# Silu stage of a fused attention and FFN kernel: the first group's z made within the last attention batches, the second's turned into another PSUM bank ahead of the first products

## The chip, the cores and the metric

The kernel runs on one core of one Trainium2 chip. The metric is the device time of one launch in microseconds (us), the median of several runs; lower is better. The profiled execution is one more run of the same program.

## The reference, cut to what matters

The activations x are 64 tiles of 128 tokens by 128 features. Eight layers follow each other, each of the form x = x + layer(layernorm(x)): a cross attention, a feed-forward network (FFN) with Silu, a cross attention, a quantised FFN, a cross attention, a gated FFN, a wide attention and a routed FFN. The change touches the first attention's last tile group and the first FFN:

```
residual = x                       # x here is already layernorm(x), the outer one
h = layernorm(x) * ln_gamma + ln_beta
w1, w2 = dequant(fc1_q, fc1_scales), dequant(fc2_q, fc2_scales)
y = silu(h @ w1 + fc1_bias)        # 128 -> 512 features
return residual + 0.5 * (y @ w2 + fc2_bias)
```

Because the layer is called on an already normalised x and adds that normalised input back, the kernel adds std2 * z to x as well as the FFN's output.

## The kernel before, in words

x stays in the on-chip memory for the whole kernel. Every layer is a "phase", written as one program for each engine. Phases are strung by one counter: VectorE (DVE) raises `phase_done` at the end of a phase, and the other engines wait for it before they begin the next. Inside a phase, each engine's order is written out by hand and semaphores join them. The tokens are worked in 16 groups of GT = 4 tiles.

**The first attention** works tile by tile (t = 0 to 63). DVE's share of tile t is, in this order (`CrossAttention.vector`, loop `body`): `normalise(t+1)` (row sums L1007, reciprocal L1009, scaling L1012, probabilities L1015), `shift(t+2)` (maxima L996, differences L999), `residual(t)` (L1021, which waits for TensorE's weighted sum of tile t, L780), then the statistics of tile t-1 for the next layer (`next_stats.tile`, L283 and L285). In the last group (t = 60 to 63, k = 0 to 3) it also calls `SiluFfn.prepare(k)`, which dequantises the FFN's weights: k = 0 scales fc1 (L1409), k = 1 fc2 and the bias (L1412 to L1416), k = 2 splits w1 into a high and a low part (L1418, L1420), k = 3 makes the bias rows (L1423 to L1431). After the loop come the statistics of tile 63, then `phase_done`. In this last group ScalarE (ACT) has one exponential for each tile (L924) and copies the turned probabilities (L916). TensorE (PE) turns the probabilities (L753) and sums them (L780).

**The Silu FFN** (`SiluFfn`, a `Hidden`) works group by group. For group g:

- DVE makes z = (x - mean) * rstd, four instructions at L346 (`vector_z`), into the one buffer `core.z`.
- PE turns z, four transposes at L1188 (`turn_z`), into PSUM bank 5.
- ACT copies it out with gamma and beta (L1256, `copy_zt`) into the one buffer `zt`; it waits until the group before has been split.
- DVE splits it in two (L1291, L1293, `split_zt`) and adds std2 * z to x, four instructions at L356 (`vector_once`, called by `keep_once`).
- PE multiplies with w1, three passes for each of four chunks: 12 matmuls at L87, L88, L89 (`hidden`), into banks 0 to 3.
- ACT applies Silu, four times L1267 (`activate`). The first of them brings a load of the function table.
- PE adds the bias by one matmul (L1441) and multiplies with w2 by 32 matmuls at L1216 (`output`), into bank 6 or 7 (`obank`).
- DVE adds the result to x (L1306, `add_output`).

TensorE's order in the steady state is: `hidden(g+1)`, `turn_z(g+2)`, `output(g)`. Ahead of it stand, in `tensor_walk`, `turn_z(0)`, `hidden(0)`, `turn_z(1)`. ACT's prologue is `copy_zt(0)`, `activate(0)`, `copy_zt(1)`. DVE's is `vector_z(0)`, `split_zt(0)`, `keep_once(0)`, `vector_z(1)`, `split_zt(1)`, `keep_once(1)`. In this layer `turn_gates`, `apply_gates` and `vector_stats` do nothing; the gated FFN, the only other `Hidden`, has its own order and its own `turn_z` and `copy_zt`.

The next attention's weights are asked for by SyncE (SP, L660) as soon as the first attention is done, so the first of these four requests also marks the moment of `phase_done`.

Of the kernel before, what the change touches and what calls it, by code (L numbers as in the profile page):

```python
# [34 lines left out]
P = 128  # L35
# [38 lines left out]
def for_groups(eng, body, peel=1):  # L74


    with eng.Fori(0, GROUPS // 2 - peel) as i:
        body(2 * i, 0, 2 * peel)
        body(2 * i + 1, 1, 2 * peel)
    for left in range(2 * peel - 1, -1, -1):  # L80
        body(GROUPS - 1 - left, 1 - left % 2, left)
# [389 lines left out]
class CrossAttention(Phase):  # L471
# [267 lines left out]
    def turn_z(self, eng, g, u, slot):  # L739
        c = self.core  # L740
        eng.wait_ge(self.ln.z_ready.sem, self.ln.z_ready.at(GT * g + GT))
        eng.wait_ge(self.t_copied.sem, self.t_copied.free(u))
        for k in range(GT):
            mm = eng.transpose(c.ps_t[:, slot, k * P:(k + 1) * P], c.z[:, k, :], c.ident[:, :])
        mm.then_inc(self.t_done.sem, 1)
# [153 lines left out]
    def copy_zt(self, eng, par, u, slot):  # L899
        c = self.core  # L900
        eng.wait_ge(self.t_done.sem, self.t_done.at(u + 1))
        if self.affine:
            eng.activation(self.zt[:, par, :], c.ps_t[:, slot, :], ACT.Identity,
                           scale=self.gb[:, 0:1], bias=self.gb[:, 1:2]).then_inc(self.t_copied.sem, 1)
        else:
            eng.activation(self.zt[:, par, :], c.ps_t[:, slot, :], ACT.Copy)\
               .then_inc(self.t_copied.sem, 1)
# [234 lines left out]
class Hidden(Phase):  # L1142
# [38 lines left out]
        return self.core.bank(6 + par)  # L1181


    def turn_z(self, eng, g, par):
        c = self.core
        eng.wait_ge(self.ln.z_ready.sem, self.ln.z_ready.at(GT * g + GT))
        for k in range(GT):
            mm = eng.transpose(c.bank(5)[:, k * P:(k + 1) * P], c.z[:, k, :], c.ident[:, :])  # L1188
        mm.then_inc(self.zt_turned.sem, 1)

    def hidden(self, eng, g, par, first=False):
# [35 lines left out]

    def tensor_walk(self, eng):
        self.turn_z(eng, 0, 0)
        self.hidden(eng, 0, 0, True)  # L1230
        self.turn_gates(eng, 0, 0, range(5))
        self.turn_z(eng, 1, 1)

        def step(g, par, left):
            if left > 0:
                self.hidden(eng, g + 1, 1 - par)
                self.turn_gates(eng, g + 1, 1 - par, (0, 1))
            if left > 1:
                self.turn_z(eng, g + 2, par)
            self.output(eng, g, par, (0, 1))  # L1240
            if left > 0:
                self.turn_gates(eng, g + 1, 1 - par, (2, 3))
            self.output(eng, g, par, (2, 3))
            if left > 0:
                self.turn_gates(eng, g + 1, 1 - par, (4,))

        for_groups(eng, step)


    def copy_zt(self, eng, g, par, first=False):  # L1250
        if not first:
            eng.wait_ge(self.zt_split.sem, self.zt_split.at(g))
        eng.wait_ge(self.zt_turned.sem, self.zt_turned.at(g + 1))
        src = self.core.bank(5)
        if self.affine is not None:
            ins = eng.activation(self.zt[:, :], src, ACT.Identity, scale=self.affine[:, 0:1],  # L1256
                                 bias=self.affine[:, 1:2])
        else:
            ins = eng.activation(self.zt[:, :], src, ACT.Copy)
        ins.then_inc(self.zt_copied.sem, 1)  # L1260
# [8 lines left out]

    def scalar_walk(self, eng):  # L1270
        self.copy_zt(eng, 0, 0, True)
        self.activate(eng, 0, 0, True)
        self.copy_zt(eng, 1, 1)

        def step(g, par, left):
            if left > 0:
                self.activate(eng, g + 1, 1 - par)
            if left > 1:
                self.copy_zt(eng, g + 2, par)
                self.stage_gates(eng, g + 2, par)  # L1280

        for_groups(eng, step)
# [28 lines left out]
            self.ln.vector_once(eng, g, par)  # L1311

    def vector_walk(self, eng):
        self.ln.vector_z(eng, 0)
        self.split_zt(eng, 0, 0)
        self.ln.vector_stats(eng, 1)
        self.keep_once(eng, 0, 0)
        self.ln.vector_z(eng, 1)
        self.apply_gates(eng, 0, 0)
        self.split_zt(eng, 1, 1)  # L1320
        self.ln.vector_stats(eng, 2)
        self.keep_once(eng, 1, 1)

        def step(g, par, left):
            if left > 1:
                self.ln.vector_z(eng, g + 2)
            if left > 2:
                self.ln.vector_stats(eng, g + 3)
            if left > 0:
                self.apply_gates(eng, g + 1, 1 - par, (0, 1))  # L1330
            if left > 1:
                self.split_zt(eng, g + 2, par)
            if left > 0:
                self.apply_gates(eng, g + 1, 1 - par, (2, 3, 4))
            if left > 1:
                self.keep_once(eng, g + 2, par)
            self.add_output(eng, g, par)

        for_groups(eng, step, 2)
        eng.wait_ge(self.added.sem, self.added.at(GROUPS))  # L1340
        eng.sem_inc(self.done.sem, 1)
# [11 lines left out]
class SiluFfn(Hidden):  # L1353
# [50 lines left out]
    def prepare(self, eng, k):  # L1404

        p, c = self.prep, self.core
        if k == 0:
            eng.wait_ge(self.loaded.sem, self.loaded.at(16 * 8))
            eng.scalar_tensor_tensor(out=self.s1[:], in0=self.q1[:], scalar=-128.0, in1=self.s1[:], op0=ALU.add,  # L1409
                                     op1=ALU.mult).then_inc(p.sem, 1)  # L1410
        elif k == 1:
            eng.scalar_tensor_tensor(out=self.s2[:], in0=self.q2[:], scalar=-128.0, in1=self.s2[:], op0=ALU.add,  # L1412
                                     op1=ALU.mult).then_inc(p.sem, 1)
            eng.tensor_scalar(self.bias[:, :], self.bias[:, :], 0.5, None, ALU.mult).then_inc(p.sem, 1)
            eng.wait_ge(p.sem, p.at(3))
            eng.tensor_scalar(self.s2[:], self.s2[:], 0.5, None, ALU.mult).then_inc(p.sem, 1)  # L1416
        elif k == 2:
            eng.tensor_copy(self.w1[0][:], self.s1[:]).then_inc(p.sem, 1)  # L1418
            eng.wait_ge(p.sem, p.at(5))
            eng.tensor_tensor(self.w1[1][:], self.s1[:], self.w1[0][:].bitcast(F32), ALU.subtract)\  # L1420
               .then_inc(p.sem, 1)
        else:
            eng.tensor_copy(self.bias_high[:, :], self.bias[:, :]).then_inc(p.sem, 1)  # L1423
            eng.tensor_scalar(self.ones[:, :], c.ident[:, :], 0.0, 1.0, ALU.mult, ALU.add).then_inc(p.sem, 1)
            eng.wait_ge(p.sem, p.at(8))
            high = self.bias_high[:, :].bitcast(F32)
            eng.tensor_tensor(self.bias_low[:, :], self.bias[:, :], high, ALU.subtract).then_inc(p.sem, 1)
            eng.tensor_scalar(self.bias_row[:, :], high, c.ident[:, 0:1], None, ALU.mult).then_inc(p.sem, 1)
            eng.wait_ge(p.sem, p.at(10))
            spread = lambda a: a[:, :].unsqueeze(1).broadcast_to([P, GT, P])  # L1430
            eng.scalar_tensor_tensor(out=self.bias_rows[:, :, :], in0=spread(self.bias_low),  # L1431
                                     scalar=c.ident[:, self.LOW:self.LOW + 1], in1=spread(self.bias_row),
                                     op0=ALU.mult, op1=ALU.add).then_inc(p.sem, 1)
# [25 lines left out]
class QuantFfn(Phase):  # L1459
# [278 lines left out]
    def tensor(self, eng):  # L1738
# [19 lines left out]
        def hidden(g, par, first=False):  # L1758
            eng.wait_ge(self.zqt_ready.sem, self.zqt_ready.at(g + 1))
            for k in range(C):  # L1760
                if not first:
                    eng.wait_ge(self.act_done.sem, self.act_done.at(C * (g - 1) + k + 1))
                eng.matmul(c.bank(k), self.wt[:, 0, k, :], self.zqt(par),
                           start=True, stop=True).then_inc(self.hid_done.sem, 1)

        turn_z(0, 0)
        turn_z(1, 1)
        hidden(0, 0, True)
        turn_z(2, 0)

        def step(g, par, left):
# [528 lines left out]
class WideAttention(Phase):  # L2300
# [74 lines left out]
    def tensor(self, eng):  # L2375
# [35 lines left out]
        def means(g):  # L2411

            self.tail.wait(eng, g)
            for k in range(GT):
                b = GT * g + k
                eng.matmul(c.bank(self.MEANS_BANK)[:, BANK - BATCH + b:BANK - BATCH + b + 1],
                           c.x[:, b, :], self.tail.rstd[:, b:b + 1], start=True, stop=True)

        prepare(0, 0, True)
        scores(0, 0, True)  # L2420

# [118 lines left out]
class RoutedFfn(Phase):  # L2540
# [254 lines left out]
    def scalar(self, eng):  # L2795
        c, U, A = self.core, self.U, self.AHEAD
        eng.wait_ge(self.before.sem, self.before.at(1))
        def copy_zt(g, par, first=False):
# [3 lines left out]
            eng.activation(self.zt[:, par, :], c.bank(6 + par), ACT.Copy).then_inc(self.zt_copied.sem, 1)  # L2802

        copy_zt(0, 0, True)
        sc = self.score[:, 0, :]
        eng.wait_ge(self.exp_go.sem, self.exp_go.at(1))
# [23 lines left out]
        def step(g, par, left):  # L2830
            for j in range(U):
                u = U * g + j
                if j < U - A or left > 0:
                    gelu(u + A, j + A)
                if j < U - A + 1 or left > 0:
                    scaled(u + A - 1, j + A - 1)
                if j == 2 and left > 0:
                    copy_zt(g + 1, 1 - par)
# [249 lines left out]
```

## Time and profile before

| | |
|---|---|
| median of 3 runs | 2571.04 us (2566.32 to 2573.92) |
| the profiled execution, whole | 2571.09 us |
| its span | 2569.3 us |
| mean granted TensorE clock | 0.939 of full speed |
| PE busy | 2287.2 us, 89% |
| DVE busy | 1869.3 us, 73% |
| ACT busy | 1459.9 us, 57% |

The span runs from the profile's first to its last instruction; some 1.8 us of the execution lie outside it. A share of busy time is a mean over all stages. The first attention ends and the Silu FFN begins near 683 us.

### The profile page before, as it was taken

Reading aid. Unit: us, or ns where it says so; the run is one execution under the profiler, and the core shown is the slowest. Engines: PE = TensorE matmul, PEld = TensorE weight load, DVE = VectorE, ACT = ScalarE, POOL = GpSimd, SP = SyncE. Lnnn points to the kernel's source line nnn. Section 1 sums busy time; section 2 is a strip of 40 time slices with the busy share of each in tenths; the row PEclk is TensorE's granted clock in tenths of the full one; section 3 lists DMA queues with packets and bytes.
Section 4 is the critical chain, followed back from the end, with each engine's and each line's share of the span. In section 5 each row is a group of like instructions: output and inputs, shape, how many; then the busy total and the mean of one; then the engine's idle time right before and its main releaser. Section 6 shows DMA issues by size and latency. Waiting matters only on the chain.

```text
span 2569.3 us, 49258 instructions
## 1 busy us (share of the span) xinstructions
PE 2287.2 (89%) x14961; PEld 1969.9 (77%) x14962; DVE 1869.3 (73%) x4436; ACT 1459.9 (57%) x2849; POOL 513.8 (20%) x700
## 2 busy tenths in 40 slices
PE   7899999999798999952458999999996998979997
PEld 6788888888597888841146888888885787879997
DVE  3778878778754888877873778888886665756665
ACT  5455565555344566624776666666663563646665
POOL 2022222222101121101001111111112341412333
PEclk9999999999899999985658999999998999989999
DMA  8444454444101444420013554545541000024444
GB/s 207 114 132 123 121 147 125 131 139 125 54 0 51 123 131 136 138 61 1 0 34 101 148 146 137 147 139 139 139 125 45 1 1 14 27 61 132 131 131 136
DMA packets 460456, 256.53 MB, mean 100 GB/s; under 512 B 25440, under 2 KB 441468, under 8 KB 460348
## 3 DMA queue, kind: packets, MB, share of 16 engines
q1 hardware_dynamic: 460348, 255.27, 35.9%
q8 instruction: 46, 0.75, 0.1%
q14 instruction: 62, 0.51, 0.1%
HBM read 150.10 MB, written 105.12 MB: 99 GB/s over the span
## 4 chain that ended last, share of the span: by engine, by line
PE 71%; DVE 13%; ACT 6%; issue 6%; POOL 1%; DVEq 1%; DMA 1%; ACTq 0%; SPq 0%; POOLq 0%
PE ps_o L780 11%; PE ps_s L764 11%; PE ps_p L87 6%; PE ps_p L88 6%; PE ps_p L89 6%; PE ps_t L753 6%; PE ps_o L1216 3%; PE ps_t L1216 2%; DVE a_sm L1007 2%; DVE a_e L1015 2%; DVE a_mx L996 2%; PE ps_s L87 2%; PE ps_t L2767 2%; PE ps_o L2767 1%; PE ps_s L89 1%
## 5 line engine op out<-in xcount | busy, mean ns | idle before, releaser
L780 PEld LDWEIGHTS ps_o<-a_val,a_pt 128*128 128x128 f32 (+2 forms) x3200 | 414.7, 193 | 35.0 <-issue 9.2
L764 PE MATMUL ps_s<-a_keys,a_zt 128*128 128x308 f32 (+1 forms) x1024 | 419.3, 494 | 14.5 <-ACT a_keys L879 6.8
L780 PE MATMUL ps_o<-a_val,a_pt 128*128 128x128 f32 (+2 forms) x3200 | 425.5, 276 | 6.7 <-ACT a_pt L916 3.9
L1007 DVE TENSOR_REDUCE a_sm<-a_e 128x16 f32<-128x1232 f32 (+1 forms) x192 | 234.3, 1220 | 226.7 <-ACT a_e L924 224.8
L888 ACT ACTIVATE a_stage<-ps_p 128x512 f32<-128x512 f32 (+1 forms) x370 | 221.1, 598 | 290.9 <-PE ps_p L89 289.8
L916 ACT ACTIVATE a_pt<-ps_t 128x512 f32<-128x512 f32 (+1 forms) x448 | 225.4, 505 | 161.7 <-PE ps_t L753 161.3
L879 ACT ACTIVATE a_keys<-ps_p 128x308 f32<-128x308 f32 x603 | 257.4, 427 | 102.5 <-PE ps_p L89 102.3
L996 DVE TENSOR_REDUCE a_mx<-ps_s 128x6 f32<-128x462 f32 (+1 forms) x512 | 255.5, 548 | 62.1 <-PE ps_s L764 41.1
L753 PE MATMUL ps_t<-ident,a_e 128*128 128x128 f32 (+1 forms) x1600 | 262.2, 276 | 31.6 <-DVE a_e L1015 29.2
L87 PE MATMUL ps_p<-ct_hi,a_mt_hi 96*128 (+1 forms) x603 | 258.9, 429 | 0.0
L1015 DVE TENSOR_TENSOR a_e<-a_e,a_rs 128x1232 f32<-128x1232 f32 (+1 forms) x192 | 251.7, 1311 | 6.6
L999 DVE TENSOR_TENSOR a_e<-ps_s,a_mx 128x462 f32<-128x462 f32 (+1 forms) x512 | 253.7, 545 | 0.0
L924 ACT ACTIVATE a_e<-a_e 128x1232 f32<-128x1232 f32 (+1 forms) x192 | 204.2, 1064 | 74.5 <-DVE a_e L999 72.4
L753 PEld LDWEIGHTS ps_t<-ident,a_e 128*128 128x128 f32 (+1 forms) x1600 | 194.8, 140 | 41.4 <-DVE a_e L1015 20.5
L764 PEld LDWEIGHTS ps_s<-a_keys,a_zt 128*128 128x128 f32 x1024 | 168.8, 190 | 42.3 <-issue 16.8
L87 PE MATMUL ps_p<-a_vo_hi,a_windowhi 96*128 96x512 f32 (+1 forms) x370 | 191.0, 516 | 0.0
L89 PE MATMUL ps_p<-ct_hi,a_mt_lo 96*128 (+1 forms) x603 | 184.2, 305 | 0.0
L88 PE MATMUL ps_p<-ct_lo,a_mt_hi 96*128 (+1 forms) x603 | 183.8, 305 | 0.0
L208 POOL TENSOR_TENSOR ln_var<-ln_mean_var,eps 128x4 f32<-128x4 f32 x48 | 9.6, 201 | 719.2 <-DVE ln_mean_var L195 710.2
L88 PE MATMUL ps_p<-a_vo_lo,a_windowhi 96*128 96x512 f32 (+1 forms) x370 | 146.9, 397 | 0.0
L89 PE MATMUL ps_p<-a_vo_hi,a_windowlo 96*128 96x512 f32 (+1 forms) x370 | 146.4, 396 | 0.0
L87 PEld LDWEIGHTS ps_p<-ct_hi,a_mt_hi 96*128 96x128 f32 x603 | 115.1, 191 | 39.3 <-issue 30.5
(392 smaller groups left out, 4675.3 us busy)
## 6 DMA issues: line engine op xcount, KB each, us to landing
a_vals<-a_stage SPq DMA_DIRECT2D x160, 512.0 KB, 3.5
a_val<-a_vals SPq DMA_DIRECT2D x128, 576.0 KB
f_w<-in_L_ffn_W_dram SPq DMA_DIRECT2D x129, 256.0 KB, 2.6
a_vals<-a_stage SPq DMA_DIRECT2D x40, 416.0 KB
a_val<-a_vals SPq DMA_DIRECT2D x64, 256.0 KB
a_val<-a_vals SPq DMA_DIRECT2D x128, 40.0 KB
x<-in_x_dram SPq DMA_DIRECT2D x8, 512.0 KB, 7.6
out_dram<-x SPq DMA_DIRECT2D x8, 512.0 KB, 5.4
```

What stands on the lines that cost most here:

```text
L87: eng.matmul(out, lhs[0], rhs[0], start=start, stop=False)
L88: eng.matmul(out, lhs[0], rhs[1], start=False, stop=False)
L89: return eng.matmul(out, lhs[1], rhs[0], start=False, stop=stop)
L753: mm = eng.transpose(c.ps_t[0:w, slot, (i % GT) * P:(i % GT + 1) * P], src[:, P * i:P * i + w], c.ident[:, :])
L764: mm = eng.matmul(o, zt, keys[:, h0:h0 + nh, :], start=True, stop=not self.masked)
L780: mm = eng.matmul(c.ps_o[:, (i % 2) * P:(i % 2 + 1) * P], self.pt[0:r, n, :], self.val[0:r, i % 2, n, :], start=(n == 0), stop=(n == self. ...
L879: eng.activation(self.keys[:, par, :, h, :], bank[:, 0:GCOLS].rearrange("p (b k) -> p b k", b=GT), ACT.Copy)\
L916: mm = eng.activation(dst[:, i0:full, :], src[:, 0:full - i0, :], ACT.Copy)
L996: eng.tensor_reduce(self.mx[:, h0:h0 + nh], bank, AX.X, ALU.max).then_inc(self.max_ready.sem, 1)
L999: eng.tensor_tensor(dest, src, bc(self.mx[:, h0:h0 + nh], KEYS), ALU.subtract)\
L1007: eng.tensor_reduce(self.sm[:, :], e, AX.X, ALU.add).then_inc(st.sem, 1)
L1015: eng.tensor_tensor(e, e, bc(self.rs[:, :], KEYS), ALU.mult).then_inc(self.probs_ready.sem, 1)
```

## The change

`prepare(1)` also makes z of group 0; `prepare(2)` also adds std2 * z to group 0's x and takes over all that `prepare(3)` did; `prepare(3)` is empty. In the Silu FFN, group 1's z is turned into bank 7 (`obank(1)`) instead of bank 5, and its place on all three engines moves ahead of the first products: TensorE turns group 1 before `hidden(0)`, ACT copies it before `activate(0)`, and DVE makes z of group 1 as soon as group 0 is turned, before it splits group 0.

```diff
+    def tbank(self, g):
+
+        return self.obank(1) if isinstance(g, int) and g == 1 else self.core.bank(5)
+
     def turn_z(self, eng, g, par):
...
-            mm = eng.transpose(c.bank(5)[:, k * P:(k + 1) * P], c.z[:, k, :], c.ident[:, :])
+            mm = eng.transpose(self.tbank(g)[:, k * P:(k + 1) * P], c.z[:, k, :], c.ident[:, :])
...
     def tensor_walk(self, eng):
         self.turn_z(eng, 0, 0)
+        self.turn_z(eng, 1, 1)
         self.hidden(eng, 0, 0, True)
-        self.turn_gates(eng, 0, 0, range(5))
-        self.turn_z(eng, 1, 1)
...
     def copy_zt(...)
-        src = self.core.bank(5)
+        src = self.tbank(g)
...
     def scalar_walk(self, eng):
         self.copy_zt(eng, 0, 0, True)
+        self.copy_zt(eng, 1, 1)
         self.activate(eng, 0, 0, True)
-        self.copy_zt(eng, 1, 1)
...
     def vector_walk(self, eng):
-        self.ln.vector_z(eng, 0)
+        eng.wait_ge(self.zt_turned.sem, self.zt_turned.at(1))
+        self.ln.vector_z(eng, 1)
         self.split_zt(eng, 0, 0)
-        self.ln.vector_stats(eng, 1)
-        self.keep_once(eng, 0, 0)
-        self.ln.vector_z(eng, 1)
-        self.apply_gates(eng, 0, 0)
         self.split_zt(eng, 1, 1)
-        self.ln.vector_stats(eng, 2)
         self.keep_once(eng, 1, 1)
...
     def prepare(self, eng, k):       # k == 1, at its end
             eng.tensor_scalar(self.s2[:], self.s2[:], 0.5, None, ALU.mult).then_inc(p.sem, 1)
+
+            self.ln.vector_z(eng, 0)
         elif k == 2:
+            self.keep_once(eng, 0, 0)
             eng.tensor_copy(self.w1[0][:], self.s1[:]).then_inc(p.sem, 1)
...
-        else:
             eng.tensor_copy(self.bias_high[:, :], self.bias[:, :]).then_inc(p.sem, 1)
```

## Rows read from the trace of the kernel before

**Rows 1.** The page's first part: busy time, share, instructions of each engine.
```profile
PE 2287.2 (89%) x14961; PEld 1969.9 (77%) x14962; DVE 1869.3 (73%) x4436; ACT 1459.9 (57%) x2849; POOL 513.8 (20%) x700
```
**Rows 2.** Chain that ended last, 640 to 730 us: start, us, what.
```profile
671.25 0.43 DVE f_w L1416
671.67 1.36 DVE a_sm L1007
...
695.85 0.50 PE ps_s L87
```
**Rows 3.** Timeline of DVE, 668 to 706: start, us, instruction, idle before it.
```profile
676.02 0.69 DVE L1420 TENSOR_TENSOR f_w1lo<-f_s,f_w1hi 128x512 fp32r<-128x512 f32 x1
680.51 0.29 DVE L1021 TENSOR_TENSOR x<-ps_o,x 128x128 f32<-128x128 f32 x1 [3.79 <-PE ps_o L780]
...
681.13 0.19 DVE L1423 CAST f_b_high<-f_b 128x128 fp32r<-128x128 f32 x1
...
682.69 0.28 DVE L283 BATCH_NORM_STATS2 tail_stats<-x 128x6 f32<-128x128 f32 x1
...
683.21 1.11 DVE L346 TENSOR_SCALAR z<-x,tail_mean_var,tail_rstd 128x128 f32<-128x128 f32 x4
686.48 0.43 DVE L1291 CAST f_zthi<-f_zt 128x512 fp32r<-128x512 f32 x1 [2.16 <-ACT f_zt L1256]
...
687.55 1.13 DVE L356 SCALAR_TENSOR_TENSOR x<-z,a_std,x 128x128 f32<-128x128 f32 x4
688.79 1.11 DVE L346 TENSOR_SCALAR z<-x,tail_mean_var,tail_rstd 128x128 f32<-128x128 f32 x4
```
**Rows 4.** Timeline of PE, 675 to 706.
```profile
676.93 3.54 PE L780 MATMUL ps_o<-a_val,a_pt 128*128 128x128 f32 x20
684.46 1.09 PE L1188 MATMUL ps_t<-ident,z 128*128 128x128 f32 x4 [3.99 <-DVE z L346]
687.69 0.79 PE L87 MATMUL ps_s<-f_zthi,f_w1hi 128*128 128x512 f32 x1 [2.14 <-DVE f_ztlo L1293]
...
692.98 0.61 PE L1188 MATMUL ps_t<-ident,z 128*128 128x128 f32 x4
695.85 0.50 PE L87 MATMUL ps_s<-f_zthi,f_w1hi 128*128 128x512 f32 x1 [2.27 <-DVE f_ztlo L1293]
...
700.30 0.60 PE L1188 MATMUL ps_t<-ident,z 128*128 128x128 f32 x4
```
**Rows 5.** Timeline of all engines, 655 to 716.
```profile
664.03 2.39 PE L780 MATMUL ps_o<-a_val,a_pt 128*128 128x128 f32 x20
...
683.07 0.35 SPq L660 DMA_DIRECT2D a_wq<-in_L_xattn_Wq_dram  x1
...
704.47 0.48 PE L87 MATMUL ps_s<-f_zthi,f_w1hi 128*128 128x512 f32 x1
...
707.35 0.60 PE L1188 MATMUL ps_t<-ident,z 128*128 128x128 f32 x4
```
**Rows 6.** Timeline of ACT, 668 to 706.
```profile
669.92 1.23 ACT L924 ACTIVATE a_e<-a_e 128x1232 f32<-128x1232 f32 x1 [0.68 <-DVE a_e L999]
...
685.67 0.78 ACT L1256 ACTIVATE f_zt<-ps_t,f_gb 128x512 f32<-128x512 f32 x1 [8.06 <-PE ps_t L1188]
689.42 1.28 ACT L1267 ACT_TABLE_LOAD   x1 [2.97 <-PE ps_s L89]
...
693.18 0.69 ACT L1267 ACTIVATE f_hid<-ps_p,f_b 128x512 f32<-128x512 f32 x1 [0.55 <-PE ps_p L89]
```
**Rows 7.** Windows: stretch, length, busy of each engine, granted clock, DMA share, GB/s.
```profile
689.50:693.00 3.50, 3.50 (x10) 2.56 (x9) 0.41 (x2) 3.11 (x4) 0.00 (x0) 0.50 0.00 0
693.00:696.40 3.40, 1.13 (x7) 0.83 (x6) 1.80 (x5) 1.36 (x2) 0.00 (x0) 1.00 0.00 0
696.40:699.80 3.40, 3.40 (x9) 2.64 (x8) 1.53 (x6) 1.52 (x3) 0.00 (x0) 0.50 0.03 7
...
701.00:800.00 99.00, 99.00 (x691) 90.16 (x690) 53.98 (x150) 44.42 (x71) 0.00 (x0) 1.00 0.00 0
```

## The prediction, made before the changed kernel ran

> **What bounds the kernel now.** The page's busy shares come first: TensorE is busy 89% of the span and DVE 73% [rows 1]. That is a mean over eight stages, and the change touches one seam, so the stage's own rows decide. I read the chain that ended last around 683 us, then the timelines of DVE, PE and ACT one by one, then the granted clock by windows.
>
> Three regimes meet at the seam. In the attention's last tiles the chain runs through DVE: the fc2 scaling of `prepare(1)` ends, and the row sums of tile 63 start at once behind it [rows 2]. Tile 63's exponential had ended at 669.92 + 1.23 = 671.15 [rows 6], so those row sums wait for DVE's queue and not for ACT. Then comes a prologue in which one engine at a time works. From 701 us on PE is busy in all of the 99.00 us looked at, at full clock [rows 7]: there nothing but PE's own work sets the pace: 99.00 us for 691 matmuls at 49 a group (12, 4, 1 and 32) is 7.0 us a group. So microseconds won before 701 reach the stage's end whole; the steady state has no slack on PE to swallow them. The next stage begins when this one ends, and its weights are asked for at the seam, over 100 us ahead of their use, so it moves with it.
>
> **The change, part by part.** I keep the times of the profiled execution and say what each edit adds to or takes from the path.
>
> *1. z of group 0 in `prepare(1)`.* Four instructions at L346 take 1.11 us [rows 3]. They go in between the end of L1416 and the row sums of tile 63, on the path, where nothing covers them: the exponential is only some 0.4 us ahead of its use. Cost +1.1. The inputs (x and the statistics of group 0) have been ready for long, so it waits for nothing. Behind it in DVE's queue stand tile 63's row sums and probabilities, and PE waits for these: its turned probabilities and the last weighted sum move by 1.1 too. Bounds: +0.7, if the 0.4 hid a part, which the chain speaks against, and +1.2.
>
> *2. `keep_once(0)` and the bias rows in `prepare(2)`.* DVE ends L1420 at 676.71 and then stands idle 3.79 us until PE's last weighted sum lets the residual go at 680.51 [rows 3]. Into that gap go four L356 (1.13 us) and the old `prepare(3)`, which lasts from 681.13 to 682.69, 1.56 us [rows 3]: 2.7 us of work. The weighted sum moves by the same 1.1 as the start of the gap, so the gap keeps its 3.8 us and 1.1 us are left over. Cost nothing. Without that cover, whatever runs over 3.8 us would delay the residual one for one; if the sum ended 1.05 us sooner (20 matmuls in 2.39 us as at 664 instead of 3.54 [rows 4, 5]), it would just fit.
>
> *3. `prepare(3)` empty.* It stands between the statistics of tile 62 and those of tile 63, all on the path. Gain 1.56, from 681.13 to 682.69 [rows 3].
>
> *4. `vector_z(0)` off the seam.* Before, the stage was declared done by 683.07, when SP issues its first request [rows 5], and the first transpose came at 684.46 [rows 4], behind z. Now z is there already, and PE begins about as soon as SP did, give or take a tenth: 683.2 to 683.3. Gain 1.2 (1.1 to 1.4).
>
> *5. `vector_z(1)` ahead of `split_zt(0)`.* The transposes of group 0 end at 685.55; ACT's copy runs 685.67 to 686.45 and the split follows at 686.48 [rows 3, 6]. DVE now waits for the end of the transposes too and spends 1.11 us on z of group 1, so the split begins about 1.25 behind the transposes' end instead of 0.93. Cost +0.3, between nothing and 0.5. The new wait for `zt_turned` holds only work that depends on it anyhow. The second transposes, 1.09 us at half clock, end within a tenth of the split's own end, so `hidden(0)` behind them on PE hardly waits.
>
> *6. The stall between `hidden(0)` and `hidden(1)`.* Call the start of `hidden(0)` X; before it is 687.69. `hidden(0)` runs to X + 5.3 = 692.98; then come four transposes, an idle 2.27 us, and `hidden(1)` at 695.85 [rows 4]. The idle time is one engine after another: transposes, copy at 693.8 once the four Silu are done, split. Now ACT copies group 1 at X (it waits for the first split), to X + 0.8; DVE splits to X + 2.0. That is 3.3 us before PE needs it. ACT's Silu of group 0 are not later, since the table load waits for the first chunk at X + 1.73 [rows 6] and the copy is over by X + 0.8. So `hidden(1)` follows `hidden(0)` directly. Gain 695.85 - 692.98 = 2.87. It also needs Silu (0, c) for chunk c: 1.28 of table load and four of 0.69 (pitch 0.64) from X + 1.73 put the last at X + 5.7 to 6.2, chunk by chunk ahead of PE. `output(0)`, `turn_z(2)` and `split_zt(2)` keep their old distance behind `hidden(1)`, and z of group 2 is ready by X + 4.4.
>
> *7. The clock.* `hidden(0)` still had 0.50 in the row up to 693.0; from there it was 1.00, when PE had been busy without a gap for 5 us, and 0.50 again from 696.4, after the idle gap before `hidden(1)`; from 699.8 it stays 1.00 [rows 7]. These are the levels 1.2 and 2.4 GHz. `hidden(1)` took 700.30 - 695.85 = 4.45 us [rows 4]; the same twelve matmuls at full clock take 707.35 - 704.47 = 2.88 [rows 5]. With no gap before it the clock should not fall again. Gain 1.57. `hidden(0)` itself took 5.29 where full clock takes 2.88, so it could gain from 0 to 2.4 if the clock rises sooner; since PE now does the second transposes just ahead of it, some 1.2 us more of gapless work, I take a rise 1.2 us earlier, which is worth 1.2 x (5.29 - 2.88) / 5.29 = 0.5.
>
> The trace thus has the clock fall after a gap and rise after gapless work. The Trainium skill (TensorE: Matmul & The Clock Gate, Part 1) says the same, but adds that the moment is run-variable, so that one kernel shows a different number of slow matmuls from run to run, and warns against fitting a specific count. By the rows the clock gives 2.1 us; by the page that term should be left unsized, and the sum would be 2.1 smaller. One trace cannot show how it varies.
>
> *The last attention tile.* PE's idle time before tile 63 grows from 2.5 to 3.6 us. Its weighted sum already ran mostly at half clock, 3.54 us against 2.39 [rows 4, 5]; all at half clock, by the ratio 5.29 / 2.88 that item 7 gives, it would take 4.39, so it may lose up to 0.85, or gain up to 1.15. The middle is near nought, which I take.
>
> **Sum:** +1.1 - 1.56 - 1.2 + 0.3 - 2.87 - 1.57 - 0.5 = -6.3 us. Against the profiled execution's own 2571.09, which stands at the runs' median of 2571.04, that is **2564.8 us**.
>
> **The rivals.**
>
> *A, the clock gives more.* `hidden(0)` mostly at full clock (another 1.9) or the last weighted sum at full clock (1.1). For it: nothing but 1.2 us of transposes now lies before X and no gap. Against: the same gapless stretch needed 5 us before. Time about 2562.5.
>
> *B, the stall stays.* The second split comes late, because ACT's copy waits for the first split, the turn waits for z, and each sits in a hand-written queue; PE then still idles before `hidden(1)` and the clock falls again. Only items 1 to 5 count: -1.4, so 2569.7. Against it stand 3.3 us of slack.
>
> *C, DVE's new load at the seam costs more.* The four L356 and the bias rows, with their waits, outlast the gap, or the small instructions do not fit in: 1 to 2 us late, so 2566.5. Against it: 1.1 us left over.
>
> *D, slower.* The granted clock stays at half through the whole prologue and two outputs. PE's longer gap before tile 63 leads in, and the full clock that PE had from 693.0 to 696.4 is lost. Price: `hidden(0)` and `hidden(1)` at half are 10.6 us instead of the 7.7 of the sum, 2.9 more. Transposes, bias and the 32 matmuls of an output take 704.47 - 700.30 = 4.17 us at full clock [rows 4, 5], and by the ratio 1.84 another 3.5 at half. It decides for slower only once the half clock lasts to X + 18, the end of the first output: 2.9 + 3.5 just makes up for the 6.3. Through the next group too (2.4 + 3.5) it gives 2577, while nothing in the trace has PE busy that long at half.
>
> **How the numbers follow.** Chances: the forecast (5 to 7.7 us less) 0.48, A 0.27, B 0.11, C 0.10, D 0.04. 0.3% is 7.7 us, about what a measurement of this kernel can tell from no change. The forecast falls 1.4 us short of it; the three runs of before lie 7.6 us apart, so about a quarter of the forecast's share and most of A's come out beyond it: faster 0.36. B, C and the rest of the forecast are within: 0.60. Slower 0.04. The range goes from A with both clock terms, 2561.8, to B, 2569.7, each widened for the spread of a median: 2559 to 2570.5. It leaves out D and the far tails of A.
>
> **What would show it.** Right: no L1423 to L1431 after the last residual, and these with four L356 in DVE's gap before it; the first L1188 within 0.3 us of SP's first request; eight L1188 before the first L87; 24 matmuls L87 to L89 without a gap, the later twelve in about 2.9 us; first L1441 some 8.5 us behind X instead of 13. Wrong: idle time before `hidden(1)`; a granted clock of 0.50 in it; a residual of tile 63 that starts well behind the end of PE's last sum; a second table load; a group period other than 7 us after the prologue.

## The result, and the profile after

The changed kernel takes 2562.67 us (median of 7 runs, 2556.63 to 2565.35), against 2571.49 us for the kernel before (7 runs): 8.8 us less. The ratio is 0.9964, 95% interval 0.9951 to 0.9977, that is 0.23% to 0.49% less time. Forecast were 2564.8 us and 6.3 less; the range held the time. The likeliest single case was "within 0.3%"; the ratio lies just beyond that bound and its interval reaches to both sides of it. The 8.8 us also lie outside the forecast's own band of 5 to 7.7 us less, and the median stands at rival A's 2562.5.

I measure the change by a **seam** that every profile shows: from the start of tile 61's residual (the third last L1021) to the first addition of an FFN output. Before, it lasts 704.97 - 669.80 = 35.17 us. The line numbers have moved: L1188 is now L1192, L1256 is L1259, L1291 and L1293 are L1294 and L1296, L1267 is L1270, L1306 is L1309.

The timeline of DVE in the changed kernel, answering to [rows 3]:

```profile
670.70 0.43 DVE L1415 TENSOR_SCALAR f_w<-f_w 128x512 f32<-128x512 f32 x1
671.04 1.11 DVE L346 TENSOR_SCALAR z<-x,tail_mean_var,tail_rstd 128x128 f32<-128x128 f32 x4
672.07 1.44 DVE L1007 TENSOR_REDUCE a_sm<-a_e 128x16 f32<-128x1232 f32 x1
...
676.07 1.11 DVE L356 SCALAR_TENSOR_TENSOR x<-z,a_std,x 128x128 f32<-128x128 f32 x4
...
679.07 0.75 DVE L1432 SCALAR_TENSOR_TENSOR f_bias_rows<-f_b_low,ident,f_b_row 128x512 fp32r<-128x512 f32 x1
680.70 0.29 DVE L1021 TENSOR_TENSOR x<-ps_o,x 128x128 f32<-128x128 f32 x1 [0.88 <-PE ps_o L780]
...
681.33 0.27 DVE L283 BATCH_NORM_STATS2 tail_stats<-x 128x6 f32<-128x128 f32 x1
...
682.48 1.11 DVE L346 TENSOR_SCALAR z<-x,tail_mean_var,tail_rstd 128x128 f32<-128x128 f32 x4 [0.66 <-PE ps_t L1192]
683.50 0.43 DVE L1294 CAST f_zthi<-f_zt 128x512 fp32r<-128x512 f32 x1
...
685.50 0.43 DVE L1294 CAST f_zthi<-f_zt 128x512 fp32r<-128x512 f32 x1 [0.85 <-ACT f_zt L1259]
...
696.63 0.69 DVE L1309 TENSOR_TENSOR x<-ps_t,x 128x512 f32 x1 [0.86 <-PE ps_t L1220]
```

z of group 0 stands between L1415 and the row sums (671.04). The bias rows are through at 679.8, 0.9 us before PE's last sum lets the residual go. The statistics of tile 63 follow the residual after 0.63 us instead of 2.18. The second split is done by 686.7, long before PE asks for it.

The timeline of PE in the same kernel, answering to [rows 4]:

```profile
675.59 2.49 PE L753 MATMUL ps_t<-ident,a_e 128*128 128x128 f32 x10 [3.48 <-DVE a_e L1015]
677.87 2.79 PE L780 MATMUL ps_o<-a_val,a_pt 128*128 128x128 f32 x20
681.72 0.66 PE L1192 MATMUL ps_t<-ident,z 128*128 128x128 f32 x4 [1.06 <-DVEq L1092]
683.65 0.66 PE L1192 MATMUL ps_o<-ident,z 128*128 128x128 f32 x4 [1.27 <-DVE z L346]
684.71 0.50 PE L87 MATMUL ps_s<-f_zthi,f_w1hi 128*128 128x512 f32 x1 [0.40 <-DVE f_ztlo L1296]
...
689.16 0.40 PE L87 MATMUL ps_s<-f_zthi,f_w1hi 128*128 128x512 f32 x1
...
691.98 0.60 PE L1192 MATMUL ps_t<-ident,z 128*128 128x128 f32 x4
```

The start of group 0's turn follows SP's first request at once; the timeline of all engines has it:

```profile
681.70 0.35 SPq L660 DMA_DIRECT2D a_wq<-in_L_xattn_Wq_dram  x1
```

The idle 2.27 us ahead of `hidden(1)` are gone (689.16), and `hidden(1)` lasts 691.98 - 689.16 = 2.82 us instead of 4.45. The windows of the granted clock, answering to [rows 7]:

```profile
685.50:688.90 3.40, 3.40 (x9) 2.62 (x8) 3.06 (x10) 3.10 (x4) 1.34 (x3) 0.50 0.33 90
688.90:692.00 3.10, 3.10 (x15) 2.43 (x14) 0.26 (x2) 2.69 (x5) 0.00 (x0) 0.99 0.02 5
692.00:800.00 108.00, 107.11 (x759) 97.82 (x757) 56.12 (x156) 45.29 (x73) 0.75 (x1) 1.00 0.00 0
```

`hidden(0)` begins at full clock, is at half clock from 685.5 to 688.9, and from there on PE stays at full clock. The seam is 696.63 - 669.25 = 27.38 us, 7.8 less. But this profiled execution (2556.63 us) was also the fastest of its seven, and 6.1 us of its 14.5 lie behind the seam (1858.2 us from there to the span's end, against 1864.3). So the first question was what belongs to the change.

### The profile page after: what moved, and what is told of

The parts are those of the page before. It is cut to its first block, busy times and chain, and to the rows that moved or that the text cites. A ratio compares the mean times of both kernels' runs of the same rounds, so it can differ in the third digit from the quotient of the medians.

```text
span 2554.8 us, 49257 instructions
## 1 busy us (share of the span) xinstructions
PE 2279.3 (89%) x14960; PEld 1963.4 (77%) x14962; DVE 1870.0 (73%) x4436; ACT 1459.3 (57%) x2849; POOL 515.2 (20%) x700
## 4 chain that ended last, share of the span: by engine, by line
PE 71%; DVE 13%; ACT 6%; issue 6%; POOL 1%; DVEq 1%; DMA 1%; ACTq 0%; SPq 0%; POOLq 0%
PE ps_o L780 11%; PE ps_s L764 11%; PE ps_p L87 6%; PE ps_p L88 6%; PE ps_p L89 6%; PE ps_t L753 6%; PE ps_o L1220 3%; PE ps_t L1220 2%; DVE a_sm L1007 2%; DVE a_e L1015 2%; DVE a_mx L996 2%; PE ps_t L2768 2%; PE ps_s L87 1%; PE ps_o L2768 1%; PE ps_s L88 1%
```

## The experiments

"Behind" is the time from the seam's end to the end of the span. Rows are from one profile each, ratios from the timed runs against the kernel before.

| kernel | seam us | tile 63, turn to residual | hidden(0) to start of hidden(1) | hidden(1) | behind | ratio, 95% interval |
|---|---|---|---|---|---|---|
| before | 35.17 | 5.40 | 8.16 | 4.45 | 1864.3 | |
| before, again | 35.22 | 5.44 | 8.19 | 4.45 | 1863.8 | |
| changed | 27.38 | 5.11 | 4.45 | 2.82 | 1858.2 | 0.9964 (0.9951 to 0.9977) |
| changed, 2nd | 27.94 | 6.30 | 3.85 | 2.81 | 1862.9 | 0.9962 (0.9948 to 0.9976) |
| changed, 3rd | 27.95 | 6.27 | 3.85 | 2.83 | 1862.8 | one run |
| changed, 4th | 27.98 | 6.31 | 3.86 | 2.80 | 1862.7 | 0.9964 (0.9951 to 0.9978) |
| order only | 30.24 | 5.27 | 4.98 | 2.80 | 1862.8 | 0.9969 (0.9958 to 0.9980) |
| prepare only | 31.84 | 5.20 | 7.33 | 4.44 | 1864.0 | 0.9992 (0.9983 to 1.0001) |
| stall filled | 33.54 | 5.36 | 8.15 | 2.89 | 1865.2 | 0.9994 (0.9984 to 1.0005) |
| clock held | 25.13 | 4.15 | 3.09 | 2.91 | 1863.1 | 0.9959 (0.9946 to 0.9972) |
| z in the gap | 25.90 | 5.17 | 3.97 | 2.80 | 1859.9 | 0.9958 (0.9945 to 0.9971) |
| z in the slots | 25.36 | 4.16 | 4.45 | 2.80 | 1863.8 | 0.9961 (0.9948 to 0.9974) |
| all moved | 26.13 | 5.32 | 4.43 | 2.81 | 1864.7 | 0.9965 (0.9951 to 0.9979) |
| all moved, clock held | 23.78 | 4.05 | 3.08 | 3.01 | 1864.3 | 0.9957 (0.9944 to 0.9971) |

**The changed kernel again**, three times.

> The changed kernel once more, for the spread. Seam: from the start of tile 61's residual to the first addition of an FFN output. It was 35.2 us in the profile of before and 27.4 in that of the changed kernel. My theory (the gain is the seam's alone, 6.3 to 7.8 us, the rest of the first 8.8 is where the granted clock happened to fall elsewhere): seam 26.5 to 28.5, whole 6 to 9 us less than before. Rival (the change also makes later stages faster): everything behind the seam again takes 5 us or more less than in the profile of before.

> The changed kernel a third time, for the spread of the seam and of the granted clock. Theory: seam 26.5 to 28.5. Rival as in the second run of it.

> The changed kernel beside the two, on the same chip and against the same runs of before. Theory: ratio 0.996, seam 27.3 to 28.0.

The three seams agree within 0.04 us, and the stretch behind is 0.9 to 1.6 us shorter than in the two profiles of before, not 6. So the seam's 7.2 to 7.8 us are the change's, and 4.6 us of the first profile's gain were that execution's own. The rival falls. The remaining 0.9 to 1.6 us behind the seam are open: over all kernels here that stretch runs from 1858 to 1865 us with no relation to the seam. Its two shortest values, 1858.2 and 1859.9, come with a mean granted clock of 0.93 in it, the other twelve with 0.92.

The later three differ from the first in one place. The timeline of PE in the second run of it, and then its window:

```profile
676.16 2.49 PE L753 MATMUL ps_t<-ident,a_e 128*128 128x128 f32 x10 [3.48 <-DVE a_e L1015]
678.44 3.98 PE L780 MATMUL ps_o<-a_val,a_pt 128*128 128x128 f32 x20
```

```profile
674.90:681.80 6.90, 5.64 (x26) 5.38 (x27) 5.34 (x15) 1.55 (x4) 0.00 (x0) 0.51 0.00 0
```

PE waits 3.48 us for tile 63's probabilities, 1.0 more than before, and in three of four executions the half clock then held over the whole weighted sum: 3.98 us instead of the 3.54 of [rows 4], and 6.3 us from the turn to the residual instead of 5.4. Half of these 0.9 us lie in the sum. The other half lies in the turning of the probabilities ahead of it: from its start to the sum's it is 2.28 us instead of 1.82, and that in all four profiles of the changed kernel.

`hidden(0)` differs too. In the second execution the granted clock was 0.50 from 685.2 and 1.00 from 688.6, so `hidden(0)` began at half clock and had full clock 2.1 us later; the third and the fourth look the same. In the first it began at full clock and lost it for 3.4 us.

**The kernel before, again.**

> The kernel before a second time, for the spread of its seam and of what lies behind it. Theory: seam 35.2 us within 0.7, and 1863 to 1865 us behind it; the changed kernel's three later profiles have 27.9 to 28.0 and 1862.7 to 1862.9. Rival (the half clock can fall into the last weighted sum here too, as it did in those three): seam 36 or more.

35.22 us and 1863.8 behind, tile 63 as in the first profile: both profiles of before show the milder case. Two profiles cannot exclude the other one.

**Order only.** The new order and bank; `prepare` as before, and `keep_once(0)` ahead of the second z.

```diff
     def vector_walk(self, eng):
+        self.ln.vector_z(eng, 0)
+        self.keep_once(eng, 0, 0)
         eng.wait_ge(self.zt_turned.sem, self.zt_turned.at(1))
         self.ln.vector_z(eng, 1)
         self.split_zt(eng, 0, 0)
```

> Only the new order and the new bank; z and std2*z of group 0 and the bias rows stay where they were, and keep_once(0) comes ahead of vector_z(1). Theory (items 5 to 7 of the prediction, which the changed kernel's profile puts at 5.6 us together): seam 29.0 to 30.5 us, whole 5 to 6 us less. Rival (the clock gives nothing, only the stall of 2.9 goes): seam 32.3, whole 3 less. Rival (the stall goes only because z of group 0 is there ahead): seam 35.

30.24 us, within what the theory gave: 4.9 less than before. The stall goes although z of group 0 is made at the seam, and the clock gives its share: 1.65 us in `hidden(1)`, but only 0.3 in `hidden(0)`, which runs at half clock nearly to its end. By the whole time too this part alone is most of the change.

**Prepare only.** The work moved into the attention's tiles; order and bank as before.

> Only the work moved into the last attention tiles; order and bank as before. Theory (items 1 to 4: +1.0 for z on the path, -1.55 for the bias rows, -1.4 for z off the seam): seam 33.3 us (32.5 to 34), whole 1.9 less, too little to be told by the whole time. Rival (the parts need each other, the stall shrinks too): seam under 32. Rival (z on the path delays PE's last sum at a lower clock and eats it all): seam 35 or more.

31.84 us, 1.5 less than the theory's 33.3 and just inside the rival's bound. But the rival's mechanism is not there. Its PE timeline still has the stall:

```profile
689.11 0.60 PE L1188 MATMUL ps_t<-ident,z 128*128 128x128 f32 x4
691.99 0.49 PE L87 MATMUL ps_s<-f_zthi,f_w1hi 128*128 128x512 f32 x1 [2.28 <-DVE f_ztlo L1293]
```

From the second turn to `hidden(1)` it is 2.88 us, as before (2.87). The extra comes from matmuls that met a full clock: `hidden(0)` with 4.45 us instead of 5.29, the first transposes with 0.66 instead of 1.09, and 0.2 in tile 63. The two parts' seams gain 4.93 + 3.33 = 8.3 us where the whole change has 7.2 to 7.8. The difference lies in the steps whose clock varies: against the later three executions it is above all tile 63, which lost 0.9 us there and in neither part; against the first, `hidden(0)`, whose gains in the parts sum to 1.15 where it had 0.84.

**Stall filled.** The kernel before with PE busy on unread transposes in the stall.

```diff
         self.turn_z(eng, 1, 1)
+        for _ in range(20):
+            eng.transpose(self.core.bank(4)[:, 0:P], self.core.ident[:, :], self.core.ident[:, :])
```

> The kernel before, with 20 transposes of the identity into the unused bank 4 put into PE's idle time between hidden(0) and hidden(1): extra work that no one reads, the stall itself stays. Theory (the gap lets the clock fall, which makes hidden(1) cost 4.45 instead of 2.9): granted clock 1.00 through hidden(1), seam 33.6 us (33.2 to 34.2), whole 1.6 less although more is done. Rival (the clock falls whatever lies in the gap, or costs nothing): seam 35.2 or, with the filler in the way, more.

33.54 us. The stall stays (8.15 us from `hidden(0)` to `hidden(1)`), yet `hidden(1)` takes 2.89 us instead of 4.45. Its timeline of PE, and then its windows:

```profile
694.15 2.35 PE L1230 MATMUL ps_p<-ident 128*128 128x128 f32 x20
696.59 0.49 PE L87 MATMUL ps_s<-f_zthi,f_w1hi 128*128 128x512 f32 x1
```

```profile
683.40:693.70 10.30, 6.35 (x16) 4.74 (x17) 4.91 (x17) 3.97 (x5) 3.80 (x8) 0.50 0.31 89
693.70:703.00 9.30, 9.21 (x68) 8.33 (x67) 5.22 (x16) 4.78 (x7) 0.00 (x0) 1.00 0.01 3
```

More work and a shorter seam: the idle gap brought the half clock that `hidden(1)` ran at, and that is worth 1.6 us apart from the stall itself. The whole time does not resolve this (0.9984 to 1.0005).

**Clock held.** The changed kernel with such transposes in every idle time of PE at the seam: 28 behind tile 62's sum, 8 behind tile 63's, 10 and 3 around the second turn. Nobody reads them.

> The changed kernel, with transposes of the identity into the unused bank 4 put into PE's idle times of the seam: 28 behind the weighted sum of tile 62, 8 behind that of tile 63, 10 and 3 around the transposes of group 1. Nobody reads them. Theory (about 1.6 us of hidden(0) and some 0.4 of tile 63 are lost to the half clock): granted clock 1.00 from tile 62 on, seam 25.3 us (24.8 to 26.2) instead of 27.4, whole 2 less than the changed kernel. Rival (the fillers are in the way or the clock stays as it is): seam 27.4 or more.

25.13 us, 2.3 to 2.9 less than the changed kernel. The windows show full clock throughout:

```profile
671.00:683.00 12.00, 11.06 (x96) 10.35 (x96) 10.99 (x33) 2.60 (x6) 0.76 (x2) 1.00 0.01 2
683.00:700.00 17.00, 16.73 (x105) 14.09 (x103) 9.46 (x29) 11.08 (x17) 3.72 (x7) 1.00 0.17 54
```

Tile 63 takes 4.15 us from the turn to the residual instead of 6.3, and `hidden(0)` gives way after 3.1 instead of 3.9. By the whole time (0.9959 against 0.9962 and 0.9964) it cannot be told from the changed kernel.

**z in the gap.** `vector_z(0)` moved from the end of `prepare(1)` to the start of `prepare(2)`.

> The changed kernel with z of group 0 made in prepare(2), in DVE's gap before tile 63's residual, instead of in prepare(1). Theory (item 1: it is on the path in prepare(1) and costs 1.0; item 2: the gap has 0.9 us left): the row sums of tile 63 follow L1415 at once, DVE is 0.1 to 0.3 late for the residual, seam 26.6 us (26.2 to 27.0), clock apart. Rival (item 1 costs nothing since tile 63 waits for something else): seam 27.4 or, with the gap overrun by the whole 1.1, 28.5.

The row sums come 1.78 us behind tile 61's residual instead of 2.82, so item 1 was on the path whole. The seam came out 0.7 lower than expected, because this execution had the full clock in tile 63. Its timeline of PE, and then that of DVE, show what the clock gave and the queue took:

```profile
673.56 3.82 PE L780 MATMUL ps_o<-a_val,a_pt 128*128 128x128 f32 x20 [1.42 <-issue]
...
680.09 2.40 PE L780 MATMUL ps_o<-a_val,a_pt 128*128 128x128 f32 x20
```

```profile
682.98 0.75 DVE L1431 SCALAR_TENSOR_TENSOR f_bias_rows<-f_b_low,ident,f_b_row 128x512 fp32r<-128x512 f32 x1
683.65 0.28 DVE L1021 TENSOR_TENSOR x<-ps_o,x 128x128 f32<-128x128 f32 x1
```

PE's sum ends at 682.49, the residual starts at 683.65 with no idle time before it: DVE is 1.1 us late. Between the statistics of tile 61 and that residual DVE had room for 3.6 us at full clock, and its work there, the split of w1 included, takes 4.7. By the slow turn and sum of the changed kernel (6.3 us instead of 4.05) the room would have been 5.8, an estimate that no run tries.

The clock was not held in this execution; its half clock lay elsewhere. The sum of tile 62 took 3.82 us here (673.56) instead of 2.47, with a granted clock of 0.50 from 673.0 to 676.4. It ended at 677.38, before DVE had tile 63's probabilities ready and came to its residual (678.34), so the half clock cost nothing there. "z in the slots" has the same (3.87 us, 0.50 from 672.8 to 675.9). One profile each does not show whether moving z brings this about or chance; so the seams of these two kernels are lower than the changed kernel's by more than what their edits move.

**z in the slots.** `vector_z(0)` two tiles at a time, where DVE idles for the exponentials.

```diff
+                if self.next_stats and self.setup and g == GROUPS - 2 and k >= 2:
+                    self.after.ln.vector_z(eng, 0, range(2 * k - 4, 2 * k - 2))
```

> The changed kernel with z of group 0 made two tiles at a time behind the residuals of tiles 58 and 59, where DVE idles 0.7 us for the exponential. Theory: 0.55 us of work fits each of these idle times, so the whole 1.0 of item 1 comes back and the gap keeps its slack: seam 26.4 us (26.0 to 26.8), clock apart, and the tiles 58 to 60 keep their period of 7.7 us. Rival (the idle time is not free, since DVE's order delays the row sums): period of tiles 59 and 60 longer by up to 0.5 each, seam 26.4 but the whole no better.

25.36 us, lower than expected again by the clock in tile 63. The next answer, DVE's timeline at the first of the two slots, shows the 0.57 us within the old 0.7 of idle time:

```profile
649.39 0.28 DVE L1021 TENSOR_TENSOR x<-ps_o,x 128x128 f32<-128x128 f32 x1
...
650.01 0.57 DVE L346 TENSOR_SCALAR z<-x,tail_mean_var,tail_rstd 128x128 f32<-128x128 f32 x2
650.77 1.44 DVE L1007 TENSOR_REDUCE a_sm<-a_e 128x16 f32<-128x1232 f32 x1 [0.20 <-ACT a_e L924]
...
657.12 0.28 DVE L1021 TENSOR_TENSOR x<-ps_o,x 128x128 f32<-128x128 f32 x1
```

The residuals stand 7.73 us apart here; in the changed kernel it is 7.73 as well. The slot is free. With the full clock the old gap just holds its load: the sum ends at 681.95, the residual starts at 682.09.

**All moved, and all moved with the clock held.** Beside z in the slots: the halvings of w2 and bias move from `prepare(1)` to `prepare(2)`, and the bias rows go behind the second split, with PE waiting for them only before its first bias matmul. The second kernel adds transposes as above (18, 8, 10, 3).

```diff
+        elif k == 4:
             eng.tensor_copy(self.bias_high[:, :], self.bias[:, :]).then_inc(p.sem, 1)
...
         self.split_zt(eng, 1, 1)
+        self.prepare(eng, 4)
         self.keep_once(eng, 1, 1)
```

> z of group 0 behind the residuals of tiles 58 and 59, the halving of w2 and of the bias moved from prepare(1) to prepare(2), and the bias rows made in the Silu FFN behind the split of group 1, with PE waiting for them only before its first bias matmul. Theory: tile 63's row sums then wait only for the exponential (1.4 us behind tile 61's residual instead of 1.8), DVE is early for the last residual whatever PE's clock, and DVE's 4 us of idle time before group 2's split hide the bias rows: 0.4 less than the run with z in the slots, seam 25.0 us (24.3 to 25.8). Rival (the bias rows delay z of group 2 and its turn): turn of group 2 later behind hidden(1), seam 26 or more.

> The same with transposes of the identity into bank 4 in PE's idle times: 18 behind tile 62's weighted sum, 8 behind tile 63's, 10 and 3 around the turn of group 1. Theory: granted clock 1.00 throughout, another 0.8 to 1.6 us less: seam 23.7 us (23.3 to 24.3), whole 10 us less than before. Rival (fillers now stand in the way, since the gap behind tile 62 is shorter): the turned probabilities of tile 63 start late, seam 25 or more.

The row sums now follow after 1.38 us (another 0.4), and the turn of group 2 still comes directly behind `hidden(1)`, so the bias rows delay nothing there. In the second kernel PE arrives sooner, and z of group 2, which ends at 688.39 + 1.16 behind the bias rows, holds its turn back to 689.60, by 0.1 us: that much of the first kernel's rival is true. The first of the two has a seam of 26.13, 0.3 above what was expected at most. That is the rival's number (26 or more) without its mechanism: in this profile the half clock held both in tile 63 (5.32) and in most of `hidden(0)` (4.43). With the clock held the seam is 23.78, as expected, 4.2 less than the changed kernel beside it. The fair comparison for the moved work alone is with "clock held", 25.13: both have full clock throughout, and 1.35 us separate them, near the 1.0 and 0.4 that the row sums show. This kernel and the changed one have 2559.20 and 2561.74 us, and intervals that overlap (0.9944 to 0.9971 against 0.9951 to 0.9978). By the seam it is the best version; by the whole time that is not shown.

## Why the prediction was right, point by point

The mechanism held in steps 1 to 6 and every step can be found; the sizes of the clock's terms did not, and two of them miss in opposite directions. Forecast, then the changed kernel's first profile, then its second (which stands for the later three); all against the first profile of before:

| step | forecast | first | second |
|---|---|---|---|
| 1 z of group 0 on the path | +1.1 | +1.03 | +1.01 |
| 2 work in DVE's gap | 0 | 0 | 0 |
| last attention tile, clock | 0 | -0.29 | +0.90 |
| 3 bias rows off the path | -1.56 | -1.55 | -1.56 |
| 4 z off the seam | -1.2 | -1.38 | -1.38 |
| 5 z of group 1 ahead of the split | +0.3 | -0.24 | -0.24 |
| 6 stall before `hidden(1)` | -2.87 | -2.87 | -2.87 |
| 7 clock in `hidden(0)` | -0.5 | -0.84 | -1.44 |
| 7 clock in `hidden(1)` | -1.57 | -1.63 | -1.64 |
| seam | -6.3 | -7.8 | -7.2 |

- Steps 1 to 3 were read off rows and came out within 0.1. "z in the gap" and "z in the slots" prove step 1 by taking it away: the row sums then follow tile 61's residual after 1.78 and 1.79 us instead of 2.82.
- Step 4 was 0.2 short: PE began 0.02 us behind SP's request (681.72 against 681.70), not 0.1 to 0.2.
- Step 5 has the mechanism right. From the end of the first transposes to the split it is 1.12 us against 0.93, so the cost is 0.2. What turned its sign is a clock term that I left out: the first transposes took 0.66 instead of 1.09.
- Step 6 is exact, and "order only" and "stall filled" separate it from the clock.
- Step 7 was in the sum at 2.1 and came to 2.5 to 3.1. `hidden(1)` is proved by "stall filled". The spread is all in `hidden(0)`: 3.85 and 4.45 us in four executions of one program. I had it at half clock from its start, with the rise 1.2 us earlier. In the later three that is the form, but the rise came 2.1 us behind the start of `hidden(0)` instead of 5.3, so 3.2 us earlier. In the first it is not: the clock was full at the start and fell only then. Why the rise came so much earlier is open.
- The last attention tile was taken at nought and spreads the other way, from -0.3 to +0.9. I had bounded the loss at 0.85, all of it in the weighted sum, which at half clock was to take 4.39 us. Measured wholly at half clock it took 3.98, a loss of 0.44; the other 0.46 came from the turning, which the prediction left out. So the bound fits by luck.
- In the later three, tile 63's loss of 0.9 cancels the 0.9 that `hidden(0)` gave beyond the forecast, which is luck too: it keeps the seam's -7.2 near the forecast's -6.3. Between the first execution and the later ones, the 0.6 that `hidden(0)` gives make up for half of the 1.2 that tile 63 costs, which is why the seams differ by only 0.6.
- The Trainium skill (TensorE: Matmul & The Clock Gate, Part 1) says that one kernel's count of slow matmuls varies from run to run. The four profiles agree; here it moves each of two steps by 0.6 to 1.2 us. By the Trainium skill's advice in the same part, not to fit a specific count, the prediction's alternative left the clock's term out; that gives -4.2 for the sum, 3.0 to 3.6 short of the measured seams.

What the runs' medians show beyond the seam's 7.2 to 7.8 is 1.0 to 1.6 us, and their interval is wider than that. The rivals: A (the clock gives more) is half true. `hidden(0)` gained 0.3 to 0.9 us beyond the forecast where A had 1.9; that the median stands at A's 2562.5 comes as much from the 1.0 to 1.6 us that the seam does not explain; B fell with the stall gone; C did not come about, with 0.9 us of DVE's gap left over where I had counted 1.1; D fell, since PE had full clock from 688.9 on.

## What to carry to other kernels

A stall of an engine on the critical path costs its own length and, on TensorE, what the matmuls behind it then take at half clock: here 2.9 us of stall carried another 1.6. When work is moved into an idle time, ask how long that idle time is at either clock of the engine that ends it; one that was 3.8 us behind the split of w1 held 2.7 us of new work with 0.9 to spare, and 3.6 us of room at full clock did not hold that split and the new work, 4.7 together. Where a gain is near the whole time's noise, choose two events at either side of the change and read their distance in several profiles: here it repeats within 0.6 us, while whole runs of one kernel spread over 8. But such a distance holds only what lies between the two events: a fall of the clock that shifts to just before the first one, or to where nothing waits for it, changes the distance as an edit would, so compare profiles in which it lies in the same place, or is held off.

## What the runs showed of the hardware that was not expected

Unread transposes in PE's idle times made the kernel's seam shorter though they are pure extra work: 28 + 8 + 10 + 3 of them brought it from 27.4 or 28.0 to 25.1 us, with the granted clock at 1.00. At full clock throughout, `hidden(1)` starts 3.1 us behind `hidden(0)` instead of 2.9: PE then waits 0.2 us, and starts when the first Silu behind the table load of 1.28 us has ended (687.94, `hidden(1)` at 687.99): the load is the next limit.

The clock fell without a long idle time too. In the changed kernel's first profile it was 1.00 from 678.7 and 0.50 from 685.5, inside `hidden(0)`, though PE's longest idle time in between was 1.27 us; in the kernel before, the falls at 675.9 and 696.4 us followed idle times of 2.46 and 2.27 us.
